# First stage of a convolution network on one core: quarter images with the channels on the partitions, and stores in rows of eight images

## What is computed

```python
def _gn(v, G=32, eps=1e-05):        # 32 groups of 1 channel: one image's channel is normalised by itself
    g = v.reshape(B_, G, C_ // G, H_, W_)
    m = jnp.mean(g, axis=(2, 3, 4), keepdims=True)
    s = jnp.var(g, axis=(2, 3, 4), keepdims=True)
    return ((g - m) / jnp.sqrt(s + eps)).reshape(v.shape)
...
x = x + _L0_conv_ref(_gn(x), L0_conv_weight, L0_conv_bias)   # 3x3, own weights at every pixel
x = x + _L1_conv_ref(_gn(x), ...)                            # 16 nearest pixels, attention, batch norm
return x
```

## Time and profile before

| what | value |
|---|---|
| runs shown | 11979.10, 11979.92 and 11986.17 us, median 11979.92 |
| profiled execution, first to last instruction (span) | 11977.8 us |
| first stage, until the convolution's first transfer is issued | 184.65 us |
| PE, DVE, ACT, POOL busy | 74%, 86%, 85%, 27% of the span |
| moved by DMA | 480.57 MB, 40 GB/s over the span |

### The profile page before, as it was taken

The page is one execution under the profiler, slowest core; times in us unless marked ns, Lnnn a source line. Parts: engine busy times, 40 slices in busy tenths (PEclk is TensorE's granted clock), DMA queues, the critical chain, the costliest instruction groups (busy, mean ns, idle before and its releaser), DMA issues. The chain is left out here.

```text
span 11977.8 us, 322272 instructions
## 1 busy us (share of the span) xinstructions
PE 8919.8 (74%) x114746; PEld 6368.8 (53%) x114746; DVE 10276.0 (86%) x23897; ACT 10163.3 (85%) x11576; POOL 3199.6 (27%) x2040
## 2 busy tenths in 40 slices
PE   2885667777777777877777777777777777777775
PEld 2664345555555555555555555555555555545553
DVE  1000599999999999999999999999999999999997
ACT  2332489999999999999999998999999999989986
POOL 0221022222222222222222222222222222222221
PEclk9887889999999999999999999999999999999998
DMA  9666800000000000000000000000000000000003
GB/s 164 172 177 175 256 16 17 17 17 16 17 17 17 17 17 16 5 17 17 17 17 16 17 17 16 16 17 16 17 17 4 17 17 17 17 16 16 17 4 132
DMA packets 267542, 480.57 MB, mean 40 GB/s; under 512 B 196964, under 2 KB 197348, under 8 KB 248356
## 3 DMA queue, kind: packets, MB, share of 16 engines
q1 hardware_dynamic: 242532, 349.99, 12.5%
q0 software_dynamic: 23424, 109.21, 2.9%
HBM read 353.59 MB, written 105.50 MB: 38 GB/s over the span
## 5 line engine op out<-in xcount | busy, mean ns | idle before, releaser
L843 POOL TENSOR_TENSOR masked<-masked,shares_a 128x784 f32<-128x784 f32 x1600 | 2988.8, 1868 | 7371.9 <-DVE rest L1159 4237.3
L1088 DVE MAX8 found<-scores 128x8 f32<-128x224 f32 x11200 | 3479.0, 370 | 223.7 <-ACT scores L990 188.9
L1017 ACT ACTIVATE turned_sb<-psum 128x512 f32<-128x512 f32 (+1 forms) x5600 | 2945.5, 572 | 507.7 <-PE psum L896 431.4
L898 PE MATMUL psum<-ident_a,masked 128*128 128x128 f32 x19200 | 2649.4, 282 | 902.8 <-ACT turned_sb L1017 860.9
L898 PEld LDWEIGHTS psum<-ident_a,masked 128*128 128x128 f32 x19200 | 2373.5, 195 | 1359.9 <-issue 1359.5
L1127 DVE CUSTOM_DVE_ANT_0 masked<-masked,scores 128x3136 f32<-128x3136 f32 x800 | 2719.1, 3399 | 0.2 <-DVE scores L1119 0.2
L990 ACT ACTIVATE scores<-psum 128x1568 f32<-128x1568 f32 x1600 | 2375.1, 1484 | 224.7 <-DVE minus_top L1127 190.0
L1002 ACT ACTIVATE masked<-masked,minus_top 128x3136 f32<-128x3136 f32 x800 | 2363.5, 2954 | 0.0
L982 ACT ACTIVATE masked<-shares_a,own 128x3136 f32<-128x3136 f32 x800 | 2328.4, 2910 | 1.0
L896 PE MATMUL psum<-ident_a,masked 128*128 128x128 f32 (+1 forms) x10400 | 1764.5, 284 | 528.7 <-ACT turned_sb L1017 494.1
L896 PEld LDWEIGHTS psum<-ident_a,masked 128*128 128x128 f32 (+1 forms) x10400 | 1106.7, 139 | 1289.1 <-issue 1213.3
(11 more groups left out here) (137 smaller groups left out, 6415.4 us busy)
## 6 DMA issues: line engine op xcount, KB each, us to landing
w_in<-in_L_conv_weight_dram POOLq DMA_DIRECT2D x392, 144.0 KB, 3.4
w_in<-in_L_conv_weight_dram SPq DMA_DIRECT2D x392, 144.0 KB, 3.5
points<-unit SPq DMA_DIRECT2D x128, 392.0 KB
shares_a<-share SPq DMA_DIRECT2D x32, 1568.0 KB
windows<-xg SPq DMA_DIRECT2D x42, 928.0 KB, 13.5
xg<-padded SPq DMA_DIRECT2D x32, 406.0 KB, 16.8
table<-table_sb SPq DMA_DIRECT2D x32, 404.2 KB
rows<-table SPq DMA_DIRECT2D x32, 396.0 KB
```

The lines of the kernel that those rows point to most:

```text
L843: nc.gpsimd.tensor_tensor(m, m, shares[:, t.half, k * width:(k + 1) * width], ALU.add).then_inc(logits_ready, 1)
L898: last = nc.tensor.matmul(out, block, ident[:], start=True, stop=True)
L1017: nc.scalar.activation(turned_sb[0:high, t.par, g * GROUP:g * GROUP + width // P, :].rearrange("p a b -> p (a b)"), ps[0:high, bank:bank + ...
L1088: n = step(nc.vector.max(found[:, t.par, c, :], scores[:, t.par, c * PART:(c + 1) * PART]))
```

## The change

`normalise_input` is written anew. A partition now holds one channel of one quarter of an image (14 rows, 784 pixels), and a block of 32 partitions holds one quarter (q = 0 to 3) of all 32 images. The whole input (100 KB for each partition) and the whole padded result (104 KB) are on chip, so that no buffer is used twice. The work goes in four chunks of eight images. SP issues everything: first 16 loads (four quarters for each chunk, each to 32 partitions, 8 pieces of 3136 bytes in each), then eight border rows, then for each chunk, when its eight images are normalised, four stores (one for each quarter). Now eight images lie side by side in `padded` as they do in `xg`, so a row of a store is 8 x 58 x 4 = 1856 bytes.

The channel's statistics now lie in four partitions: DVE takes two `bn_stats` of 392 pixels and a `bn_aggr` for each image, PE averages the means over the four quarters with a matrix of quarters, DVE adds the squared deviation of the quarter's mean to its variance, and PE averages that. These small steps are done for eight images at once. POOL makes the matrix (one `memset`, seven `affine_select`) and clears the two border columns; it starts no transfer any more. ACT normalises each image with an instruction of its own, 32 in all.

```diff
-    x_rows = x.rearrange("b c h w -> (b c) (h w)")
+    CHUNKS = 4
+    CB = BATCH // CHUNKS
+    PARTS = 2
+    PART = QN // PARTS
+    x_cols = x.rearrange("b c (q h) w -> q c b (h w)", q=PER)
...
-        x_in = enter(nc.sbuf_tensor("x_in", [P, 2, N], FP32))
-        padded = enter(nc.sbuf_tensor("padded", [P, 2, H, WP], FP32))
+        x_in = enter(nc.sbuf_tensor("x_in", [P, BATCH, QN], FP32))
+        padded = enter(nc.sbuf_tensor("padded", [P, QH, BATCH, WP], FP32))
...
         @block.gpsimd
...
-                    pool.wait_ge(normed, g + 1)
-                    pool.dma_start(x_in[:, par, :], x_rows[bass.ds(g * P, P), :]).then_inc(x_loaded[par], 16)
+            nc.gpsimd.memset(average[:], 0.0).then_inc(average_ready, 1)
+            for n, d in enumerate(range(1 - PER, PER)):
+                pool.wait_ge(average_ready, n + 1)
+                nc.gpsimd.affine_select(out=average[:], in_=average[:], compare_op=ALU.not_equal, fill=1.0 / PER,
+                                        base=C * d, pattern=[[-1, P]], channel_multiplier=1).then_inc(average_ready, 1)
+            nc.gpsimd.memset(padded[:, :, :, 0:1], 0.0).then_inc(edges_clear, 1)
+            nc.gpsimd.memset(padded[:, :, :, WP - 1:WP], 0.0).then_inc(edges_clear, 1)
...
         @block.vector
...
+            for k in range(CHUNKS):
+                at = images(k)
+                dve.wait_ge(x_loaded[k], 16 * PER)
+                for b in range(k * CB, (k + 1) * CB):
+                    for h in range(PARTS):
+                        step(nc.vector.bn_stats(stats[:, b, h, :], x_in[:, b, h * PART:(h + 1) * PART]))
+                dve.wait_ge(chain, steps[0])
+                for b in range(k * CB, (k + 1) * CB):
+                    nc.vector.bn_aggr(moments[:, b, :], stats[:, b, :, :].rearrange("p a b -> p (a b)")).then_inc(moments_ready, 1)
+                dve.wait_ge(moments_ready, CB * (k + 1))
+                dve.wait_ge(mean_made, k + 1)
+                step(nc.vector.tensor_tensor(dev[:, at], moments[:, at, 0], mean_ps[:, at], ALU.subtract))
...
+        @block.tensor
+        def _(pe):
+            pe.wait_ge(average_ready, 2 * PER)
+            for k in range(CHUNKS):
+                at = images(k)
+                pe.wait_ge(moments_ready, CB * (k + 1))
+                nc.tensor.matmul(mean_ps[:, at], average[:], moments[:, at, 0], start=True, stop=True).then_inc(mean_made, 1)
+                pe.wait_ge(second_ready, k + 1)
+                nc.tensor.matmul(var_ps[:, at], average[:], second[:, at], start=True, stop=True).then_inc(var_made, 1)
...
         @block.scalar
...
+                for b in range(k * CB, (k + 1) * CB):
+                    nc.scalar.activation(padded[:, :, b, 1:1 + W], x_in[:, b, :].rearrange("p (h w) -> p h w", w=W),
+                                         ACT.Identity, bias=shift[:, b:b + 1], scale=scale[:, b:b + 1]).then_inc(normed, 1)
...
         @block.sync
...
-                    sp.wait_ge(normed, g + 1 + x_free_credit)
-                    for j in range(PER):
-                        sp.dma_start(xg[:, 1:1 + H, bass.ds(g * PER + j, 1), :].rearrange("c h b w -> c h (b w)"),
-                                       padded[C * j:C * (j + 1), par, :, :]).then_inc(stored[par], 16)
...
+            for k in range(CHUNKS):
+                for q in range(PER):
+                    sp.dma_start(x_in[C * q:C * (q + 1), images(k), :], x_cols[q, :, images(k), :]).then_inc(x_loaded[k], 16)
+            sp.wait_ge(cleared, 2)
+            for k in range(CHUNKS):
+                for row in (0, HP - 1):
+                    sp.dma_start(xg[:, row, images(k), :].rearrange("c b w -> c (b w)"), zero_row[:, :]).then_inc(border_stored, 16)
+            for k in range(CHUNKS):
+                sp.wait_ge(normed, CB * (k + 1))
+                for q in range(PER):
+                    sp.dma_start(xg[:, 1 + q * QH:1 + (q + 1) * QH, images(k), :].rearrange("c h b w -> c h (b w)"),
+                                 padded[C * q:C * (q + 1), :, images(k), :].rearrange("p h b w -> p h (b w)")).then_inc(stored[k], 16)
+            sp.wait_ge(border_stored, 2 * 16 * CHUNKS)
+            for k in range(CHUNKS):
+                sp.wait_ge(stored[k], 16 * PER)
```

More of the change, by code:

```diff
@@ L41, in normalise_input @@
 def normalise_input(nc, x, xg):
-    x_rows = x.rearrange("b c h w -> (b c) (h w)")
+    CHUNKS = 4
[3 more added lines that the diff above has]
+    x_cols = x.rearrange("b c (q h) w -> q c b (h w)", q=PER)
     with ExitStack() as stack:
         enter = stack.enter_context
-        x_in = enter(nc.sbuf_tensor("x_in", [P, 2, N], FP32))
-        padded = enter(nc.sbuf_tensor("padded", [P, 2, H, WP], FP32))
[L48 to L52, removed]
-        eps = enter(nc.sbuf_tensor("eps", [P, 1], FP32))
-        zero_row = enter(nc.sbuf_tensor("zero_row", [C, BATCH * WP], FP32))
-        x_loaded0 = enter(nc.semaphore("n0_x_loaded0"))
-        x_loaded1 = enter(nc.semaphore("n0_x_loaded1"))
+        x_in = enter(nc.sbuf_tensor("x_in", [P, BATCH, QN], FP32))
+        padded = enter(nc.sbuf_tensor("padded", [P, QH, BATCH, WP], FP32))
+        stats = enter(nc.sbuf_tensor("stats", [P, BATCH, PARTS, 6], FP32))
+        moments = enter(nc.sbuf_tensor("moments", [P, BATCH, 2], FP32))
+        dev = enter(nc.sbuf_tensor("dev", [P, BATCH], FP32))
+        second = enter(nc.sbuf_tensor("second", [P, BATCH], FP32))
+        std = enter(nc.sbuf_tensor("std", [P, BATCH], FP32))
+        scale = enter(nc.sbuf_tensor("scale", [P, BATCH], FP32))
+        shift = enter(nc.sbuf_tensor("shift", [P, BATCH], FP32))
+        eps = enter(nc.sbuf_tensor("eps", [P, 1], FP32))
+        zero_row = enter(nc.sbuf_tensor("zero_row", [C, CB * WP], FP32))
+        average = enter(nc.sbuf_tensor("average_i", [P, P], FP32))
+        mean_ps = enter(nc.psum_tensor("mean_ps", [P, BATCH], FP32))
+        var_ps = enter(nc.psum_tensor("var_ps", [P, BATCH], FP32))
+        x_loaded = [enter(nc.semaphore(f"n0_x_loaded{k}")) for k in range(CHUNKS)]
+        stored = [enter(nc.semaphore(f"n0_stored{k}")) for k in range(CHUNKS)]
@@ L57, in normalise_input @@
         cleared = enter(nc.semaphore("n0_cleared"))
+        edges_clear = enter(nc.semaphore("n0_edges"))
+        average_ready = enter(nc.semaphore("n0_average"))
         chain = enter(nc.semaphore("n0_chain"))
         moments_ready = enter(nc.semaphore("n0_moments_ready"))
+        mean_made = enter(nc.semaphore("n0_mean"))
+        second_ready = enter(nc.semaphore("n0_second"))
+        var_made = enter(nc.semaphore("n0_var"))
         std_ready = enter(nc.semaphore("n0_std_ready"))
@@ L63, in normalise_input, with images @@
         border_stored = enter(nc.semaphore("n0_border"))
-        stored0 = enter(nc.semaphore("n0_stored0"))
-        stored1 = enter(nc.semaphore("n0_stored1"))
         block = enter(nc.Block())
-        x_loaded = [x_loaded0, x_loaded1]
-        stored = [stored0, stored1]
-        x_free_credit = 2
+        def images(k):
+            return slice(k * CB, (k + 1) * CB)
         @block.gpsimd
         def _(pool):
-            with pool.Fori(0, GROUPS // 2) as i:
-                for par in range(2):
-                    g = i * 2 + par
-                    pool.wait_ge(normed, g + 1)
-                    pool.dma_start(x_in[:, par, :], x_rows[bass.ds(g * P, P), :]).then_inc(x_loaded[par], 16)
+            nc.gpsimd.memset(average[:], 0.0).then_inc(average_ready, 1)
[5 more added lines that the diff above has]
+            nc.gpsimd.memset(padded[:, :, :, WP - 1:WP], 0.0).then_inc(edges_clear, 1)
@@ L80, in _, with step @@
         @block.vector
         def _(dve):
-            nc.vector.memset(padded[:], 0.0).then_inc(cleared, 1)
+            steps = [0]
+            def step(instruction):
+                steps[0] += 1
+                instruction.then_inc(chain, 1)
             nc.vector.memset(eps[:], EPS).then_inc(cleared, 1)
             nc.vector.memset(zero_row[:], 0.0).then_inc(cleared, 1)
[L85 to L99, removed]
@@ new lines, in _ @@
+            for k in range(CHUNKS):
[10 more added lines that the diff above has]
+                step(nc.vector.tensor_tensor(dev[:, at], moments[:, at, 0], mean_ps[:, at], ALU.subtract))
+                dve.wait_ge(chain, steps[0])
+                step(nc.vector.tensor_tensor(dev[:, at], dev[:, at], dev[:, at], ALU.mult))
+                dve.wait_ge(chain, steps[0])
+                nc.vector.tensor_tensor(second[:, at], dev[:, at], moments[:, at, 1], ALU.add).then_inc(second_ready, 1)
+                dve.wait_ge(std_ready, k + 1)
+                step(nc.vector.reciprocal(scale[:, at], std[:, at]))
+                dve.wait_ge(chain, steps[0])
+                nc.vector.scalar_tensor_tensor(shift[:, at], mean_ps[:, at], -1.0, scale[:, at],
+                                               ALU.mult, ALU.mult).then_inc(coef_ready, 1)
@@ L101, in _ @@
         @block.scalar
         def _(act):
[L103 to L114, removed]
```

(15 more changed lines are left out.)

## The result

The change ran in 11883.02 us (median of four runs, 11866.51 to 11890.8) against 11979.51 us (four runs) for the kernel before: ratio 0.9919, 95% interval 0.9905 to 0.9933. That is 96 us faster. 50 were predicted, and the range ended at 11894. The profiled execution took 11878.96 us, its span 11877.3.

The account below looks back on a forecast made before the run. The first stage, bounded by 232 B store rows, was to fall from 184.65 us to 138.0 (3.2 + 63.3 + 2.4 + 67.5 + 1.6), less 3.3 for switches: 50.0 us gained, 11930 us; range 11894 to 11952.

Parts of the forecast that it names:

- The bound of the stage: First stage: a chain of store, normalise, load, statistics, bounded by its 57344 store rows of 232 B (13.30 MB).
- Loads: First stage: 16 transfers to 32 partitions each, 12.85 MB at 203 GB/s, 63.3 us; bounds 29 and 68 us.
- the forecast's own range: Whole kernel: 11916 to 11945 us, from switches at 0 or all, transfers at 189 GB/s, and 4 us; chance 0.66.
- Stores: First stage: 7168 rows of 1856 B, 13.30 MB, taken at 67.5 us; outer ends 30 and 141.5 us.
- switches between halves: First stage: some 15 switches between partition halves, 0.44 us saved at each, 0 to 6.6 us less; taken 3.3.
- borders and landing: First stage: border rows, 0.48 MB behind the loads, 2.4 us; last bytes to the next stage's issue, 1.6 us.
- A line through two row prices: First-stage stores: from rows of 232 B and 3136 B, a 1856 B row takes 155 ns, 191 GB/s, 69.5 us.
- The rival with overlapping halves: First stage: engines drift apart, both halves work all the time at 263 GB/s; stage 106 us, total 11901; chance 0.17.
- The windows over 250 GB/s: Sign in the first stage's transfers: the forecast is wrong if windows show 250 GB/s and more.
- Compute: First stage: 12.1 to 14.6 us a chunk for statistics and chain, ACT 6.0 to 7.2, hidden behind transfers.
- Behind the stage: Stages after the first: the convolution gets the same `xg`; taken at 0, with 4 us allowed either way.
- The skill's rule on halves: First-stage transfers: two to different halves only 6% faster than one, so switches save at most 7 of 133 us.

Follow-up runs that it names:

- the version in steps: The change with a channel's quarters on neighbouring partitions, one load per chunk to 128 partitions, stores from every fourth partition: 11841.74 us, ratio 0.9892 to the kernel before.
- The order of the quarters: The change with each chunk's quarters loaded and stored in the order 0, 2, 1, 3, so every transfer switches partition half: 11860.53 us in one run.
- the kernel with 16 visits: The kernel before with first-stage statistics over eight pieces of 392 pixels instead of seven of 448; attention stage 10398.0 us, convolution begun at 179.2 us.
- The two without the path: Kernel before and change, each with attention's branch that searches a doubtful tile's scores again never taken: 11783.19 us (0.984) and 11716.83 us (0.9784).

## Why the prediction was wrong

**The bound of the stage** was right: store, normalise, load, statistics, with the 232 B rows at its root. Cutting the stores back to one image brought their pace back to 100 GB/s and the stage to 199 us.

**Loads** were right: 63.3 us at 203 GB/s, measured 208 for as long as they ran alone. So was the loss against a load to 128 partitions, which the version in steps got back (411). Two slips of the working had no effect on this: the price of a store row comes to 191 GB/s, not the 189 of the loads' bound, and the terms named for the forecast's own range give about 11923 as its lower end, not 11916.

**Stores** were mis-sized, and this is the step that failed in the stage: 67.5 us, less at most 6.6 for switches between halves. With borders and landing they took some 53 us from about 65 on, where the sum had 71.5. A line through two row prices was the lesser error: it put 2 us above the price by bytes, and one half alone stored rows of 1856 B at about 200 GB/s, near the 203 by bytes. The greater was the switches. I took 0.44 us for each from the convolution's store, where four transfers of 3.2 MB switch once. Here 16 transfers of 0.8 MB followed on loads, and as I read the paces the engines were out of step from the meeting on, with both halves at work for somewhat over a quarter of the time (an estimate: 252 is that share of the way from 203 to 380). The order of the quarters and the steps of four show that it is the halves; what breaks the step is open. The rival with overlapping halves was the right mechanism at the wrong strength: it had 106 us, and the measured 118.9 lay between it and the forecast's 134.7. The windows over 250 GB/s that were to show it are there. With other orders, queues and partitions it goes further: 103.5, 98.6 and 75.6 us.

**Compute** was right: DVE's chunk took 7.58 + 0.71 us and a chain of 4.2 in the first chunk (a table load is in it) and 2.7 later, 11.0 to 12.5 in all, against 12.1 to 14.6; ACT took 7.6 against 6.0 to 7.2, a term a little short, and covered.

**Behind the stage** failed outright: 0, with 4 us either way. It was 34.7 us. The sum said "the convolution gets the same `xg`", and that is true only to the last bits. Seven pieces of 448 became eight of 392 averaged by PE, and a branch on the data further on was taken 13 times instead of 15. 25.1 us of the 34.7 lie at the two tiles whose visits are gone. The remaining 10 us are not settled: they are within the 38 us over which the attention stage moves at an equal number of visits. The convolution, 3.4 us shorter, stayed within the 4. With either step alone right, the time would have been in the range; both went the same way.

**The skill's rule on halves.** The Trainium skill, SBUF — State Buffer, "Can I just issue two DMAs to hit both halves?", answers no, with 6% from a second transfer. The loads on one queue agree: 213 GB/s in turns, 208 in the change's order. The stores disagree, and so do the loads from two queues (293): in turns from the two halves, on one queue, the stores moved 360 GB/s where one half alone moves about 200. An estimate by the rule lets the switches save 7 us at most; they saved some 16 (69.5 us for borders, stores and landing at 203 GB/s, against 53). The same page's section "Door 1: The DMA port swizzle" says that the pace goes by how many of 16 ports the partitions reach, and that 32 neighbours reach half of them; by its formula 32 partitions in steps of four reach all 16. Their 382 GB/s agree.

## What to carry to other kernels

Ask of every transfer how long its rows are and which partitions it touches: 232 B rows moved 100 GB/s, 928 B rows 229 (both halves in part at work), and 32 partitions in steps of four moved 382 where 32 neighbours alone move about 200. Where such blocks can't be avoided, let successive stores on a queue take blocks of different halves. And where a later stage branches on data, a change in the order of a sum can be a change in time: count the visits in both traces before the time is given to the edit.

## What the runs showed that was not expected

On one queue, loads that alternated between the halves stayed at 213 GB/s, while stores in the same order reached 360; loads gained only when a second queue had the other half (293). What brings the engines out of step where stores follow loads, and lets loads keep it, was not found: it isn't the border transfers.

The attention stage, untouched in all of them, took 10345.2 us in one kernel with 13 visits and 10383.2 in another. Their mean granted clocks were 0.959 and 0.951 (two answers, one for each kernel):

```profile
core 0: 11834.8 us, clock 0.959
```

```profile
core 0: 11889.1 us, clock 0.951
```

The other eight traces lie between in the same order: 10376.3 and 10378.6 us at 0.952 and 0.951, 10363.6 to 10371.0 at 0.954 and 0.955. The kernel before, with 15 visits at 0.952, took 21.8 us more than the one with 13 at that clock, and the kernel with 16 visits had 0.956, which may be why its time hid the visit. The two without the path, 20 us apart, had 0.957 and 0.960. Whether the clock makes these differences or follows from them was not tried.
